# Ends of a kernel's four stages: without GpSimd's drain and without the second meeting of the engines, and one clear of semaphores moved into a stage

## The chip, the cores and the metric

The kernel runs on one core of a Trainium2 chip. Its five engines are TensorE (PE in the profile; PEld is its weight load), VectorE (DVE), ScalarE (ACT), GpSimd (POOL) and SyncE (SP, which here only issues transfers). A name with a q behind it (POOLq, PEldq) is that engine's sequencer: branches, waits, drains and semaphore operations, which are not counted as busy. The metric is device time in microseconds (us) of one execution. The span is the part of it from the first to the last instruction in the profile.

## What is computed

Two layers run over a stream `x` of 16 batches of 112 rows and 256 columns, with a context of 16 batches of 375 rows:

```python
x = x + L0_xattn(layernorm(x), ctx)          # 16 heads: attention over x itself and over the context, gated
x = x + L0_ffn(layernorm(x))                 # 8 experts (256 -> 512 -> 256), the best one for each row
x = x + L1_xattn(ctx, ctx, layernorm(x))     # one head of 256 over the context
x = x + L1_ffn(layernorm(x))                 # 16 experts (256 -> 1024 -> 256), 112 places each
```

A feed-forward layer sends each row to the expert with the largest router value. In the last layer an expert takes at most 112 rows.

## The kernel before, in words

`program` runs four functions, one after the other, as stages: `attention0`, `ffn0`, `attention1` and `ffn1`. Each allocates semaphores, opens a Block, and writes in it one list of instructions per engine. Inside a stage the engines meet only through semaphores: a producer adds to one, a consumer waits for a count. The stream `x` stays on chip (`xs`), so that what goes from stage to stage through memory is rows sorted by expert: `sorted0`, `made0` and `sorted1`.

- `attention0` (Block at L329) goes through the batches one by one, with five steps more than there are batches, since each engine works on another batch. GpSimd scatters the normed rows of each batch to `sorted0` with an indirect transfer (L1244), and waits for the last of them at L1250. At its end VectorE works out which expert owns each of 21 tiles (`owner_i`, `offset_i`, L739 to L748) and adds a row for the next attention (L752). SyncE loads weights for all that comes next. TensorE ends with dummy multiplications (`keep_busy`, L156).
- `ffn0` (Block at L1359) goes over 21 tiles of 128 rows. SyncE reads an offset (L1364) and loads the tile (L1370). TensorE turns it (L1478), multiplies it up (L1493) and down (L1506). GpSimd turns the row numbers into whole numbers (L1404) and scatters the result to `made0` (L1411). SyncE also loads eight blocks of weights for `ffn1`. At the end GpSimd and SyncE both wait for the last scatters, and SyncE then loads the first batch of `made0` for the stage behind (L1393). TensorE ends with 24 dummy multiplications.
- `attention1` (Block at L1549) goes over the batches again. VectorE adds `made0` to the stream (L1703) and norms it. GpSimd first makes constants (L1166 to L1175), later scatters rows to `sorted1` (L1244). At the end SyncE waits for the last scatter and then loads the rows of the first two experts (L1591), still inside the stage, since their buffers are outside it. TensorE ends with 22 dummy multiplications.
- `ffn1` (Block at L1872) goes over 16 experts. TensorE turns the rows (L1973), multiplies up (L1988) and down (L2002), VectorE forms the output rows (L1954), and GpSimd scatters them to the output (L1919) and at last waits for the last two of these transfers (L1924 and L1925).

```python
        def phase(run, *args):

            g.phase_sems = []
            run(*args)
            if g.used_sems:
                nc.clear_and_free_semaphores(g.used_sems)
            nc.all_engine_barrier()
            g.used_sems, g.phase_sems = g.phase_sems, None
```

Nothing plans the order of the work: it is the order of the lists. Each of SyncE's transfers is issued in its order behind the waits that stand ahead of it there, and GpSimd's indirect transfers have a queue of their own.

Of the kernel before, what the change touches and what calls it, by code (L numbers as in the profile page):

```python
# [124 lines left out]
def program(nc, a, out):  # L125
    with ExitStack() as ctx:
        g = Shared()
        g.nc = nc

        def sb(name, shape, dt=F32, where=ctx):  # L130
            return where.enter_context(nc.sbuf_tensor(name, shape, dt))
# [4 lines left out]
                g.phase_sems.append(handle)  # L136
            return handle

        g.phase_sems, g.used_sems = None, []

        def phase(run, *args):

            g.phase_sems = []
            run(*args)
            if g.used_sems:
                nc.clear_and_free_semaphores(g.used_sems)  # L146
            nc.all_engine_barrier()  # L147
            g.used_sems, g.phase_sems = g.phase_sems, None

        def dram(name, shape, dt=F32):  # L150
            return nc.dram_tensor(name, shape, dt, kind="Internal").ap()
# [42 lines left out]
        with ExitStack() as layer0:  # L194
            g.w1 = sb("w1", [P, E0, 2, F0], F32, layer0)
            g.stacks = sb("stacks", [P, 3, STACK], F32, layer0)
            g.b1 = sb("b1", [P, E0, F0 // P], F32, layer0)
            g.owner_i = sb("owner_i", [1, TILES], I32, layer0)
            g.offset_i = sb("offset_i", [1, TILES], I32, layer0)
            ffn0_views(g)  # L200
            phase(attention0, nc, a, g)
            phase(ffn0, nc, a, g)
        g.x_first = [sb(f"e1_x_in{k}", [C1, ROW1]) for k in range(2)]
        phase(attention1, nc, a, out, g)
        phase(ffn1, nc, a, out, g)

def ffn0_views(g):

    k2 = F0 // P  # L210
    late = g.stacks[:, 1:3, :].rearrange("p s n -> p (s n)")
    g.w2 = late[:, 0:E0 * k2 * D].rearrange("p (e k d) -> p e k d", e=E0, k=k2)
    last = g.stacks[:, 0, :]
    at = 0

    def part(words, pattern=None, **sizes):
        nonlocal at
        view = last[:, at:at + words]
        at += words
        assert at <= STACK  # L220
        return view.rearrange(pattern, **sizes) if pattern else view

    g.weights = {n: part(2 * D, "p (k d) -> p k d", k=2) for n in ("Wk", "Wv", "Wq", "Wo")}
    g.b2 = part(E0 * D, "p (e d) -> p e d", e=E0)
    g.b1_rows = part(P)[0:E0 * k2, :]
    g.bq, g.bv = part(2), part(2)

def attention0(nc, a, g_):
# [3 lines left out]
    with ExitStack() as phase:  # L233
# [92 lines left out]
        s_ctx = [sem(f"ctx_loaded{p}") for p in range(2)]  # L326
        s_stack = [sem(f"stack_ready{p}") for p in range(3)]
        s_mr = [sem(f"max_ready{p}") for p in range(2)]
        block = phase.enter_context(nc.Block())  # L329

        def copy_queries(engine, b, part):
            for t in range(NT):
# [998 lines left out]
def ffn0(nc, a, g):  # L1331
# [3 lines left out]
    with ExitStack() as phase:  # L1335
# [5 lines left out]
        with ExitStack() as tiles:  # L1341
# [14 lines left out]
            def tile_steps(engine, step):  # L1356
                steps(engine, step, TILES, 6, TILES - 3, end, 4)

            block = nc.Block()  # L1359
            with block:  # L1360
                @block.sync
                def _(sp):
# [33 lines left out]
                def _(pool):  # L1396
                    def step(j):
# [7 lines left out]
                        if (j - 1).real():  # L1405
# [6 lines left out]
                                                    in_=y[n.parity][:, :], in_offset=None, bounds_check=N - 1,  # L1412
                                                    oob_is_err=False).then_inc(s_out[n.parity], 16)

                    tile_steps(pool, step)
                    pool.wait_ge(s_out[0], 16 * ((TILES + 1) // 2))
                    pool.wait_ge(s_out[1], 16 * (TILES // 2))
# [95 lines left out]
def attention1(nc, a, out, g):  # L1513
# [3 lines left out]
    with ExitStack() as phase:  # L1517
# [28 lines left out]
        minus_wg = sb("minus_wg", [P, 2, E1])  # L1546
        expd, sums = sb("expd", [T, E1]), sb("sums", [T, 1])
        r = batch_routing(nc, g, phase, E1, C1, "r1", lambda n: bank[7][0:T, n.rows(E1)], s["logits_mm"], bank[6][0:T, 2 * T:2 * T + E1], acc, s["expd"], 4)
        block = nc.Block()  # L1549
        with block:  # L1550
            @block.sync
            def _(sp):
# [304 lines left out]
def ffn1(nc, a, out, g):  # L1857
# [7 lines left out]
    with ExitStack() as experts:  # L1865
        def tb(name, shape, dt=F32):
            return [g.sb(f"e1_{name}{p}", shape, dt, experts) for p in range(2)]
# [1 line left out]
        x_in = g.x_first + [g.sb(f"e1_x_in{k}", [C1, ROW1], F32, experts) for k in (2, 3)]  # L1869
        index = [g.sb(f"e1_index{k}", [C1, 1], I32, experts) for k in range(4)]  # L1870
        xt, hid, y = tb("xt", [P, 2, C1]), tb("hid", [P, KF, C1]), tb("y", [C1, D])
        block = nc.Block()  # L1872
        with block:  # L1873
            @block.sync
            def _(sp):
# [148 lines left out]
```

## Time and profile before

| what | value |
|---|---|
| time of the kernel, median of 3 runs | 772.79 us (769.84 to 773.85) |
| time of the profiled execution | 771.14 us |
| its span, from the first to the last instruction | 769.3 us |
| TensorE busy | 720.3 us, 94% of the span |
| VectorE, ScalarE, GpSimd busy | 419.7, 325.5 and 218.0 us |
| mean granted TensorE clock, as a share of full speed | 0.971 |

The profiled execution is one of its own. Busy time counts an engine's work, not its waits. A line of a group of instructions has the shortest, the median and the longest duration in nanoseconds, and the starts of the first and the last one in microseconds from the start of the span. A line of the timeline has the start and the duration in microseconds, and in brackets how long the engine had been idle and what released it.

### The profile page before, as it was taken

To read this page: it belongs to the slowest core of one execution; us is meant where nothing else is said; L and a number is where in the kernel's file an instruction comes from. 1 tells how busy PE (TensorE), PEld (TensorE's weight loads), DVE (VectorE), ACT (ScalarE), POOL (GpSimd) and SP (SyncE) were. 2 spreads that over 40 slices of the span, in tenths; PEclk is the share of its full clock that TensorE was granted. 3 is DMA by queue.
4 is the path that set the end of the run, shared out by engine and by line. 5 is a ranking of instruction groups with operands and counts; after the bars stand their busy time and mean duration, and the time that the engine had idled before them with its cause. 6 is when DMAs were issued, how large, how long until landed. Compare 5 with 4: busy or idle time off the path is not lost. (4 is left out here: it accounts for less than half of the span.)

```text
span 769.3 us, 19472 instructions
## 1 busy us (share of the span) xinstructions
PE 720.3 (94%) x6739; PEld 569.3 (74%) x6740; DVE 419.7 (55%) x1269; ACT 325.5 (42%) x884; POOL 218.0 (28%) x359
## 2 busy tenths in 40 slices
PE   5789999999999999999997898998999989999995
PEld 4457667777667776667665698997788878999994
DVE  4556877778877778776763322222588861111111
ACT  1335665555665556655553143331455540110110
POOL 3212333313333213243110023333356531111111
PEclk8979999999999999999999799999999998999998
DMA  6737554345653446642535459853566633999950
GB/s 173 197 98 195 139 144 107 91 126 166 173 150 103 126 139 174 170 124 74 177 117 156 123 184 259 212 171 104 168 202 217 198 105 111 309 327 342 332 160 17
DMA packets 99527, 128.12 MB, mean 167 GB/s; under 512 B 23394, under 2 KB 84683, under 8 KB 99312
## 3 DMA queue, kind: packets, MB, share of 16 engines
q1 hardware_dynamic: 90193, 115.07, 51.2%
q0 software_dynamic: 3824, 8.46, 3.6%
q10 hardware_dynamic: 5423, 3.48, 1.9%
q8 instruction: 50, 0.82, 0.5%
q14 instruction: 37, 0.30, 0.1%
HBM read 74.68 MB, written 23.88 MB: 128 GB/s over the span
## 5 line engine op out<-in xcount | busy, mean ns | idle before, releaser
L564 ACT ACTIVATE probs<-psum 128x448 f32<-128x448 f32 (+2 forms) x256 | 125.2, 541 | 57.9 <-PE psum L917 57.4
L776 DVE TENSOR_REDUCE neg_max<-psum 112x2 f32<-112x750 f32 x128 | 118.7, 928 | 6.5 <-PE psum L900 4.7
L900 PE MATMUL psum<-stacks 96*128 96x487 bf16 (+1 forms) x256 | 75.5, 377 | 4.6 <-DVE neg_max L777 2.6
L917 PE MATMUL psum<-stacks 102*128 102x112 bf16 (+1 forms) x1024 | 76.9, 214 | 1.6 <-ACT probs L564 0.4
L932 PEld LDWEIGHTS psum<-probs,rings 128*32 128x32 f32 (+2 forms) x2048 | 44.9, 109 | 45.2 <-issue 36.8
L917 PEld LDWEIGHTS psum<-stacks 102*128 102x128 bf16 (+1 forms) x1024 | 54.4, 98 | 30.4 <-ACT probs L564 23.8
L932 PE MATMUL psum<-probs,rings 128*32 128x112 f32 (+2 forms) x2048 | 75.8, 265 | 0.0
L1954 DVE SCALAR_TENSOR_TENSOR e_y<-psum,e_x_in 112x256 f32<-112x256 f32 x16 | 7.7, 484 | 98.0 <-PE psum L2002 98.0
L1988 PEld LDWEIGHTS psum<-e_xt,rings 128*128 128x128 f32 x512 | 59.5, 192 | 2.2 <-ACT e_xt L1934 1.3
L1988 PE MATMUL psum<-e_xt,rings 128*128 128x112 f32 x512 | 59.7, 275 | 0.9 <-ACT e_xt L1934 0.9
L2002 PE MATMUL psum<-rings,e_hid 128*112 128x256 f32 x256 | 57.9, 379 | 1.3 <-DVE e_hid L1961 1.3
L987 PE MATMUL psum<-rings 128*128 128x375 f32 x128 | 48.3, 500 | 5.6 <-ACT xt L575 5.6
L2002 PEld LDWEIGHTS psum<-rings,e_hid 128*112 128x112 f32 x256 | 44.0, 177 | 10.4 <-issue 1.7
L777 DVE TENSOR_REDUCE neg_max<-psum 112x2 f32<-112x224 f32 x128 | 48.4, 378 | 0.0
L1934 ACT COPY e_xt<-psum 128x224 f32<-128x224 f32 x16 | 5.5, 345 | 99.9 <-PE psum L1973 99.9
L1438 ACT ACTIVATE t_hid<-psum,b 128x128 f32<-128x128 f32 x84 | 26.2, 363 | 50.9 <-PE psum L1493 50.9
L1493 PEld LDWEIGHTS psum<-t_xt,t_w 128*128 128x128 f32 x336 | 41.9, 197 | 5.7 <-issue 3.7
L1493 PE MATMUL psum<-t_xt,t_w 128*128 128x128 f32 x336 | 42.8, 283 | 3.4 <-issue 2.7
L1919 POOL DMA_INDIRECT out<-e_y,e_index x16 | 15.2, 951 | 98.7 <-issue 52.8
L444 POOL TENSOR_TENSOR ln_rstd<-ln_mv,eps 112x1 f32<-112x1 f32 x16 | 3.0, 190 | 138.4 <-DVE ln_mv L647 138.4
L1411 POOL DMA_INDIRECT made<-t_y,t_index x21 | 24.2, 1151 | 59.0 <-issue 45.0
L1506 PE MATMUL psum<-stacks,t_hid 128*128 x168 | 40.5, 386 | 0.0
(228 smaller groups left out, 1392.3 us busy)
## 6 DMA issues: line engine op xcount, KB each, us to landing
rings<-in_L_ffn_w SPq DMA_DIRECT2D x32, 1024.0 KB, 7.7
stacks<-rings SPq DMA_DIRECT2D x96, 243.5 KB
ct_dram<-rings SPq DMA_DIRECT2D x16, 375.0 KB, 4.9
a_ct<-ct_dram SPq DMA_DIRECT2D x16, 375.0 KB, 4.4
a_ctx<-in_ctx SPq DMA_DIRECT2D x16, 375.0 KB
stacks<-q_parts SPq DMA_DIRECT2D x93, 56.0 KB
rings<-in_ctx SPq DMA_DIRECT2D x16, 256.0 KB
w<-in_L_ffn_W SPq DMA_DIRECT2D x8, 512.0 KB, 6.2
```

The source lines that it names most:

```text
L564: nc.scalar.activation(probs[k % 4][0:keys, :, :], src, ACT.Exp, scale=DH ** -0.5).then_inc(s["exp_done"], 1)
L776: nc.vector.tensor_reduce(neg_max[:, 0, h:h + 2], psum[0:T, pair:pair + 2, 0:S], AX, ALU.max, negate=True)
L777: nc.vector.tensor_reduce(neg_max[:, 1, h:h + 2], psum[0:T, pair:pair + 2, S:KV], AX, ALU.max, negate=True).then_inc(s["max_done"], 1)
L900: last = nc.tensor.matmul(bank[2 - 2 * (k % 2) + j][0:rows, 0:KV], q_flat[n.third][0:QK, h * T:h * T + rows], k_stack[n.third][0:QK, h, :] ...
L917: last = nc.tensor.matmul(bank[4 + k % 2][0:wide, j * T:(j + 1) * T], k_flat[n.third][:, first:first + wide], q_stack[n.third][:, h, :], s ...
L932: last = nc.tensor.matmul(bank[6 + g // 2][32 * j:32 * j + 32, col:col + T], v[n.parity][0:keys, chunk, h, :], probs[k % 4][0:keys, j, :], ...
L987: last = nc.tensor.matmul(bank[(0, 3)[h]][:, 0:S], w_p[:, a_, 2, h, :], ct[b.parity][:, a_, :], start=(a_ == 0), stop=(a_ == 1))
L1438: nc.scalar.activation(hid[j.parity][:, f, :], up_bank(j, f)[:, f % 2 * P:(f % 2 + 1) * P], ACT.Relu, bias=bias).then_inc(s["hid"], 1)
L1493: last = nc.tensor.matmul(up_bank(j, f)[:, f % 2 * P:(f % 2 + 1) * P], w1_now[j.parity][:, k, f * P:(f + 1) * P], xt2[j.parity][:, k, :], ...
L1506: last = nc.tensor.matmul(bank[6 + n.parity][:, 0:D], hid[n.parity][:, f, :], w2[:, bass.ds(e, 1), f, :].rearrange("p o d -> p (o d)"), st ...
L1988: last = nc.tensor.matmul(bank[2 * e.parity + f // 4][:, f % 4 * C1:(f % 4 + 1) * C1], g.ring1[e.quarter][:, k, f * P:(f + 1) * P], xt[e.p ...
L2002: last = nc.tensor.matmul(bank[6 + n.parity][0:C1, 0:D], hid[n.parity][:, f, :], g.ring2[n.quarter][:, f, :], start=(f == 0), stop=(f == K ...
```

## The change

```diff
@@ program
-        g.phase_sems, g.used_sems = None, []
-
-        def phase(run, *args):
-
-            g.phase_sems = []
-            run(*args)
-            if g.used_sems:
-                nc.clear_and_free_semaphores(g.used_sems)
-            nc.all_engine_barrier()
-            g.used_sems, g.phase_sems = g.phase_sems, None
+        g.phase_sems = None
...
-            phase(attention0, nc, a, g)
-            phase(ffn0, nc, a, g)
+            g.phase_sems = g.first_sems = []
+            attention0(nc, a, g)
+            g.phase_sems = None
+            ffn0(nc, a, g)
         g.x_first = [sb(f"e1_x_in{k}", [C1, ROW1]) for k in range(2)]
-        phase(attention1, nc, a, out, g)
-        phase(ffn1, nc, a, out, g)
+        attention1(nc, a, out, g)
+        ffn1(nc, a, out, g)
@@ attention0
-        block = phase.enter_context(nc.Block())
+        block = phase.enter_context(nc.Block(no_gpsimd_drain=True))
@@ ffn0
-            block = nc.Block()
+            block = nc.Block(no_gpsimd_drain=True)
...
+                    nc.clear_and_free_semaphores(g.first_sems)
                     tile_steps(pool, step)
@@ attention1
-        block = nc.Block()
+        block = nc.Block(no_gpsimd_drain=True)
@@ ffn1
-        block = nc.Block()
+        block = nc.Block(no_gpsimd_drain=True)
```

## Rows read from the trace of the kernel before

**Rows 1.** The page's first part: busy time, share and instructions of each engine.

```profile
PE 720.3 (94%) x6739; PEld 569.3 (74%) x6740; DVE 419.7 (55%) x1269; ACT 325.5 (42%) x884; POOL 218.0 (28%) x359
```

**Rows 2.** Windows, last three stages: from:to, length, each engine's busy time, clock, DMA.

```profile
432.30:527.40 95.10, 89.42 (x606) 83.22 (x606) 23.54 (x42) 31.84 (x105) 28.28 (x42) 0.96 0.62 178
527.40:643.40 116.00, 107.61 (x748) 92.14 (x748) 78.52 (x352) 53.12 (x193) 54.22 (x102) 0.97 0.55 167
643.40:769.35 125.95, 116.76 (x804) 105.91 (x804) 16.32 (x32) 12.76 (x32) 18.30 (x32) 0.98 0.74 241
```

**Rows 3.** Line L233, window 429 to 434: end of `attention0`, its first meeting.

```profile
L233 PEldq DRAIN  x1: 5042/5042/5042, 427.1 to 427.1; - x1
...
L233 POOLq DRAIN  x1: 1380/1380/1380, 430.4 to 430.4; - x1
...
L233 SPq EVENT_SEMAPHORE  x1: 17/17/17, 432.3 to 432.3; - x1
```

**Rows 4.** Line L147, window 429 to 434: the second meeting behind `attention0`.

```profile
L147 SPq EVENT_SEMAPHORE  x1: 17/17/17, 432.6 to 432.6; - x1
```

**Rows 5.** Timeline, start of `ffn0`.

```profile
433.62 7.19 SPq L1370 DMA_DIRECT2D t_in<-sorted  x6
...
435.91 0.18 POOL L1404 CAST t_index<-t_in 128x1 int32<-128x1 f32 x1 [7.37 <-DMA t_in<-sorted]
```

**Rows 6.** Line L1360, window 524 to 529: end of `ffn0`, its first meeting.

```profile
L1360 PEldq DRAIN  x1: 2175/2175/2175, 524.9 to 524.9; - x1
...
L1360 POOLq DRAIN  x1: 1774/1774/1774, 525.4 to 525.4; - x1
...
L1360 SPq EVENT_SEMAPHORE  x1: 17/17/17, 527.4 to 527.4; - x1
```

**Rows 7.** Line L146, window 526 to 529: GpSimd clears `attention0`'s semaphores.

```profile
L146 POOLq DRAIN  x1: 223/223/223, 527.4 to 527.4; - x1
L146 POOLq EVENT_SEMAPHORE_RANGE_CLEAR  x1: 614/614/614, 527.7 to 527.7; - x1
```

**Rows 8.** Line L147, window 524 to 529: the second meeting behind `ffn0`.

```profile
L147 SPq EVENT_SEMAPHORE  x1: 17/17/17, 528.5 to 528.5; - x1
```

**Rows 9.** Timeline, end of `ffn0` and start of `attention1`.

```profile
525.31 0.36 SPq L1393 DMA_DIRECT2D empty<-made  x1
...
528.63 0.42 DVE L1703 TENSOR_TENSOR xs<-xs,empty 112x256 f32<-112x256 f32 x1 [6.34 <-PEq L147]
```

**Rows 10.** Tile `empty`, window 520 to 535: its two loads' time to landing.

```profile
DMA to landing us min/median/max: 2.0/2.8/3.6
```

**Rows 11.** Line L1550, window 640 to 645: end of `attention1`, its first meeting.

```profile
L1550 PEldq DRAIN  x1: 2173/2173/2173, 641.0 to 641.0; - x1
...
L1550 POOLq DRAIN  x1: 1374/1374/1374, 641.9 to 641.9; - x1
```

**Rows 12.** Timeline, end of `attention1` and start of `ffn1`.

```profile
641.68 0.79 SPq L1591 DMA_DIRECT2D e_x_in<-sorted  x2
...
644.02 0.68 PE L156 MATMUL psum<-ident 128*128 128x128 f32 x4 [0.90 <-PEq L147]
...
644.55 0.18 POOL L1912 CAST e_index<-e_x_in 112x1 int32<-112x1 f32 x1 [4.50 <-DMA e_x_in<-sorted]
```

**Rows 13.** Line L1873, window 765 to 770: end of `ffn1`, its first meeting.

```profile
L1873 POOLq EVENT_SEMAPHORE  x2: 17/17/17, 768.4 to 768.5; - x2
...
L1873 POOLq DRAIN  x1: 1372/1372/1372, 767.0 to 767.0; - x1
L1873 SPq EVENT_SEMAPHORE  x1: 17/17/17, 768.6 to 768.6; - x1
```

**Rows 14.** Line L147, window 765 to 770: the second meeting behind `ffn1`.

```profile
L147 PEldq EVENT_SEMAPHORE  x1: 51/51/51, 769.3 to 769.3; - x1
```

**Rows 15.** Windows as in rows 2: two stretches at the lower granted clock.

```profile
437.50:440.90 3.40, 2.75 (x15) 2.35 (x13) 0.69 (x1) 1.51 (x5) 0.00 (x0) 0.50 0.30 83
...
632.10:638.90 6.80, 6.80 (x34) 6.80 (x35) 3.15 (x23) 1.57 (x7) 1.92 (x2) 0.50 0.12 35
```

## The prediction

> **What bounds the kernel now.** I read the page's first part first. TensorE is busy for 94% of the span [rows 1], so that only an idle stretch of it, or the time behind its last work, can be won without making its work shorter. The windows by stage say the same of the last three stages: it is busy for 89.4 of 95.1, 107.6 of 116.0 and 116.8 of 126.0 us [rows 2]. Nothing inside a stage is edited but one clear of semaphores, so each stage's length stays if its start moves as a whole. What I must read, then, is each of the four ends: when the last engine arrives at the meeting, when it is released, and what the next stage's first work waits for besides that release.
>
> The first end is late because of TensorE, not GpSimd. GpSimd's drain begins at 430.4 and takes 1.38 us, to 431.8, while TensorE's ends at 427.1 + 5.04 = 432.1. The release is at 432.3 [rows 3], the second one at 432.6 [rows 4]. SyncE's first load of `ffn0` goes out at 433.6, and GpSimd, idle for 7.37 us, gets that tile at 435.9 [rows 5]. The second end has both drains level: GpSimd 525.4 + 1.77 = 527.2, TensorE 524.9 + 2.18 = 527.1, release 527.4 [rows 6]. Then the sequencer of GpSimd drains for 0.22 us and clears for 0.61 us [rows 7], and the second release comes at 528.5 [rows 8]. VectorE starts `attention1` 0.1 us behind it, at 528.63, and the trace names the meeting as what it waited for [rows 9]. The third end has the drains level again: 641.0 + 2.17 = 643.2 and 641.9 + 1.37 = 643.3 [rows 11]. Here the loads for `ffn1` were issued at 641.68, ahead of both meetings, and GpSimd's first work there waits for that load, not for a meeting, until 644.55 [rows 12]. At the last end nothing follows: GpSimd's drain begins at 767.0 and takes 1.37 us, release 768.6 [rows 13], and the last instruction of the kernel is the second meeting's, from 769.3 to 769.35 [rows 14].
>
> **The change part by part.** *First end.* The drain of 1.38 us goes, but TensorE's still ends at 432.1, so it is worth nothing. The second meeting goes: 432.6 - 432.3 = 0.3 us [rows 3, 4]. The new kind of meeting is not in the trace. Its nearest row is the exchange of the old one: GpSimd's two semaphore operations begin 0.1 us apart, and SyncE is released 0.1 us behind [rows 13]. If a plain drain can't itself add to the semaphore and a separate operation must, that is one such step more, 0.1 us; if it is leaner, up to 0.1 us less. I take half a step more, since drain and count were one instruction before: gain 0.25 us, between 0.2 and 0.4. The load of the first tile waits for nothing but the release, so the gain moves all of `ffn0`.
>
> *The moved clear.* It now stands in GpSimd's list ahead of the first tile. Its price is that of the rows behind `ffn0`, 0.22 + 0.61 = 0.84 us [rows 7], or less by the drain. Behind it on GpSimd is queued the wait for the first tile, and for that tile the engine idles 7.37 us [rows 5], of which 435.9 - 432.6 = 3.3 us lie behind the release. So 0.84 us is hidden at least three times over, and I cost it at nothing. Without that cover it would delay only GpSimd's row numbers, which are needed for its own scatters. It issues no transfer and passes no queue of SyncE's.
>
> *Second end.* The drain: 0.1 us between the two engines, about what a further step costs, so nothing. The clear and the second meeting: 528.5 - 527.4 = 1.1 us [rows 6, 8]. What is late next? The first batch of `made0` is loaded from 525.31 [rows 9], and loads into that buffer take 2.0 us at the least [rows 10]. It has thus landed at 527.3 if it is that one, just ahead of the release at 527.4. I take the whole 1.1 us; if it took the median's 2.8 us it would land at 528.1 and only 0.4 us would be won, but VectorE's wait was put down to the meeting and not to the load. Bounds 0.4 and 1.25 us. All loads of `attention1` are issued behind the release and move with it.
>
> *Third end.* Clear and second meeting are worth some 0.5 us on paper, since TensorE's dummy multiplications start at 644.02, 0.8 us behind the end of the drains [rows 11, 12]. But the rows land when they land: their load is issued inside the stage, and GpSimd gets them only at 644.55. Cover: the load's flight, 641.68 to about 644.5. I cost it at a gain of nothing, upper bound 0.2 us, because the dummies would be out of the way when the rows land.
>
> *Last end.* From the start of GpSimd's drain at 767.0 to the last instruction's end at 769.35 are 2.35 us. Of this the exchange of one meeting stays, 768.6 - 768.4 = 0.2 us [rows 13, 14]. Gain 2.15 us, with half a step more for the new meeting 2.1. No work and no transfer is in its way: the last output has landed before the drain begins. Bounds 2.0 and 2.2 us.
>
> **Sum.** 0.25 + 0 + 1.1 + 0 + 2.1 = 3.45, say 3.5 us. Against the profiled execution's own 771.14 us, of which 1.8 us lie outside its span of 769.3, that gives 767.6 us. The median of the runs shown lies 1.65 us above that execution, so on the scale of the medians I forecast 772.79 - 3.5 = 769.3 us. The unknown costs put the gain between 0.2 + 0.4 + 0 + 2.0 = 2.6 and 0.4 + 1.25 + 0.2 + 2.2 = 4.05 us. By about 0.5%, 3.9 us, a measurement of this kernel can tell a change from none, so the forecast sits just inside that, and most of what is uncertain is on which side it falls. The three runs shown are themselves 4 us apart.
>
> **A drain that is only put off.** No row shows what follows the span; 1.8 us of the profiled time lie around it. If GpSimd's engine has to finish what its drain did before the execution counts as over, 1.37 us [rows 13] comes back outside the span: gain 3.5 - 1.4 = 2.1 us, time 770.7. For it: the drain took 1.37 to 1.77 us at each of the four ends [rows 3, 6, 11, 13], even where the last transfer had landed, so it is work of its own and not a wait for data. Against it: the meeting's own releases need no such drain, and the only drain of GpSimd shown right behind a long one took 0.22 us [rows 7], so that most of the cost may go with the kind of drain and not with the engine's state. Chance 0.15. The Trainium skill, Runtime: NRT & Kernel Launch, section The ~15µs preamble/postamble breakdown, puts a meeting of all engines and a reset of the DMA rings behind every kernel. By that rule a drain left out could be paid there; no row here shows it.
>
> **The release is not what the next stage waits for.** If at the first two ends a transfer sets the start, as it does at the third, the 1.35 us of these two vanish and only the last end's 2.1 us are won: 770.7. The third end speaks for it [rows 12]; that VectorE starts 0.1 us behind the release [rows 8, 9] and that `ffn0`'s load is issued behind it speak against it. Chance 0.1.
>
> **TensorE's clock.** The granted clock was 0.50 of full, the 1.2 GHz level, in two stretches among others: 3.4 us, a few microseconds into `ffn0`, and 6.8 us at the end of `attention1`, where TensorE had short idle gaps between small products [rows 15]. In the second one 34 products kept it busy for 6.8 us, 0.20 us each, against 0.144 over the stage [rows 2, 15]. By the level itself such a stretch costs at most half its length, and that only where TensorE sets the pace. Moved starts can move these stretches. If the one in `ffn0` no longer falls on products, up to 1.7 us more is won: gain 5.2, time 767.6; chance 0.1. The other way is the case on the slow side. Place: the start of `ffn1`, where the dummies now end earlier, while the rows land when they did, so that TensorE idles some 0.5 us more in one piece just ahead of its longest run of products. Price: a stretch as long as the two of [rows 15] together, 10.2 us, at half clock, 5.1 us lost, less the 3.5 won: 1.6 us slower, 774.4. It decides from 7 us of low clock on, at which 3.5 us are lost. Against it: total idle there doesn't grow, it only moves, and the clock was full in that place before. Chance 0.05. The Trainium skill, TensorE: Matmul & The Clock Gate, Part 1, says that recent activity decides the clock, and by that rule alone the shorter gaps at the first two ends could only help.
>
> **The change doesn't do what it says.** The option could leave a drain of GpSimd in place, or the meeting through semaphores could cost as much as the old two. Then only the clears go: about 0.8 us at the second end and 0.4 at the last, time 771.6. Chance 0.05.
>
> **How the numbers follow.** Forecast 0.55, put-off drain 0.15, transfers set the start 0.1, clock for it 0.1, clock against it 0.05, no effect 0.05. The range holds forecast and both cases at 770.7, the bounds of the sum (768.7 to 770.2), the favourable clock at 767.6, and some 1 us of scatter of a median on both sides; it leaves out the slow side and part of the favourable clock: 766.8 to 771.9. Faster by over 0.5% is below 768.9: two fifths of the forecast's 0.55, nearly all of the 0.1 of the favourable clock, and 0.05 of the rest through scatter, 0.37. Slower by over 0.5%: half of the unfavourable clock and scatter, 0.04. The rest, 0.59, is within.
>
> **What would show it right or wrong.** Right: GpSimd's sequencer has no drain of over 1 us at any of the four ends; TensorE's drains of 5.0, 2.2 and 2.2 us are still there; one meeting per end; `ffn0` starts its first load 0.25 us earlier against TensorE's drain; VectorE's first addition of `attention1` follows that drain by 0.4 to 0.5 us in place of 1.5; `ffn1`'s first product does not follow its load's issue sooner; from GpSimd's wait for the last output to the last instruction 0.4 us in place of 2.5. The span shrinks by 3.5 us and the time outside it stays at 1.8. Wrong: the time outside the span grows by over 1 us (the put-off drain), VectorE's first addition waits for its load, GpSimd's first row numbers of `ffn0` come later than its tile, or the granted clock at the start of `ffn1` is 0.5.

## The result, and the profile after

The changed kernel takes 768.35 us, the median of 12 runs (766.89 to 770.67), against 772.0 us for 12 runs of the kernel before (768.65 to 777.28). The ratio is 0.9956, 95% interval 0.9934 to 0.9977: 3.4 us less, between 1.8 and 5.1. A second set of 12 runs, further down, gave 0.9968 (0.9949 to 0.9988). The profiled execution took 767.21 us, with a span of 765.4 (765.36): 1.8 us outside it, as in the profiled execution before.

Line numbers in the kernel after differ: the first stage's end is L226 (L233 before), the moved clear L1408, the ends of `ffn0`, `attention1` and `ffn1` are L1353, L1544 and L1867, the dummy products L147, the last wait for an output L1919.

The first end, for [rows 3, 4, 5]: the instructions of L226, of the moved clear L1408, and the timeline of the start of `ffn0`.

```profile
L226 PEldq EVENT_SEMAPHORE  x2: 51/51/51, 431.7 to 431.9; - x2
L226 POOLq EVENT_SEMAPHORE  x2: 17/17/17, 431.8 to 431.9; - x2
L226 PEldq DRAIN  x1: 5162/5162/5162, 426.4 to 426.4; - x1
...
L226 POOLq COMPARE_BRANCH  x1: 38/38/38, 429.6 to 429.6; - x1
...
L226 SPq EVENT_SEMAPHORE  x1: 17/17/17, 431.9 to 431.9; - x1
...
L1408 POOLq DRAIN  x1: 217/217/217, 431.9 to 431.9; - x1
L1408 POOLq EVENT_SEMAPHORE_RANGE_CLEAR  x1: 614/614/614, 432.2 to 432.2; - x1
...
432.91 2.58 SPq L1363 DMA_DIRECT2D t_in<-sorted  x3
...
434.97 0.44 PE L1472 MATMUL psum<-ident,t_in 128*128 128x128 f32 x2 [1.37 <-DMA t_in<-sorted]
435.09 0.18 POOL L1397 CAST t_index<-t_in 128x1 int32<-128x1 f32 x1 [7.21 <-DMA t_in<-sorted]
```

GpSimd has no drain at L226. TensorE's drain still ends the wait, at 426.4 + 5.16 = 431.6. A second thing is new in the rows: TensorE now has two semaphore operations there. Its drain no longer adds to the semaphore itself; an operation of its own does so at 431.7, and the release follows at 431.9. So SyncE's release has ended 0.32 us behind TensorE's drain, where it was 0.17 before. GpSimd's clear is over at 432.8, 2.3 us ahead of its first row numbers.

The second end, for [rows 6, 8, 9].

```profile
L1353 PEldq DRAIN  x1: 2173/2173/2173, 524.7 to 524.7; - x1
...
525.11 0.36 SPq L1386 DMA_DIRECT2D empty<-made  x1
...
527.26 0.42 DVE L1697 TENSOR_TENSOR xs<-xs,empty 112x256 f32<-112x256 f32 x1 [5.19 <-PEq L1353]
```

VectorE begins 0.40 us behind the end of TensorE's drain (526.87), where it was 1.54 before. It still waits for the meeting and not for its rows, which were asked for 2.15 us earlier.

The third end, for [rows 11, 12]: the timeline of the end of `attention1` and the start of `ffn1`, first two rows of before that [rows 12] leaves out, then the kernel after.

```profile
644.54 0.36 PE L1973 MATMUL psum<-ident,e_x_in 112*128 112x112 f32 x2
...
645.34 0.92 PE L1988 MATMUL psum<-e_xt,rings 128*128 128x112 f32 x6 [0.43 <-ACT e_xt L1934]
```

```profile
639.46 0.79 SPq L1585 DMA_DIRECT2D e_x_in<-sorted  x2
...
642.17 0.68 PE L147 MATMUL psum<-ident 128*128 128x128 f32 x4 [0.42 <-PEq L1544]
642.54 0.18 POOL L1906 CAST e_index<-e_x_in 112x1 int32<-112x1 f32 x1 [4.71 <-DMA e_x_in<-sorted]
...
642.69 0.36 PE L1967 MATMUL psum<-ident,e_x_in 112*128 112x112 f32 x2
...
643.49 0.92 PE L1982 MATMUL psum<-e_xt,rings 128*128 128x112 f32 x6 [0.43 <-ACT e_xt L1928]
```

Here something moved that I had held fixed. TensorE's last dummies end at 641.76, 2.3 us behind the issue of the row load; before it was 1.45 us (643.13 against 641.68). So the meeting came later as seen from the load, and the first expert product (L1982, at 643.49) follows the load's issue by 4.02 us, against 3.66 before. In both kernels TensorE goes from its four dummies to the rows (L1973, L1967) without an idle gap, 0.52 us behind the dummies' start, and the first expert product stands 1.3 us behind that start. So what TensorE waits for here is the meeting that releases the dummies, before the change too; the wait for the load in [rows 12] is GpSimd's.

The last end, for [rows 13, 14]: first GpSimd's last wait for an output before, then the rows after.

```profile
L1925 POOLq EVENT_SEMAPHORE  x1: 17/17/17, 766.8 to 766.8; - x1
```

```profile
L1919 POOLq EVENT_SEMAPHORE  x1: 17/17/17, 764.9 to 764.9; - x1
...
L1867 POOLq EVENT_SEMAPHORE  x2: 17/17/17, 765.2 to 765.3; - x2
...
L1867 PEldq EVENT_SEMAPHORE  x1: 51/51/51, 765.3 to 765.3; - x1
```

From GpSimd's last wait to the last instruction it is 0.42 us, against 2.55 before.

The windows of the last three stages, for [rows 2], and of the low clock, for [rows 15]; columns as there.

```profile
431.90:527.10 95.20, 89.62 (x606) 83.37 (x606) 23.57 (x42) 31.85 (x105) 27.92 (x42) 0.96 0.64 177
527.10:642.10 115.00, 107.44 (x748) 92.16 (x748) 78.62 (x352) 53.13 (x193) 54.25 (x102) 0.97 0.56 171
642.10:765.36 123.26, 116.75 (x804) 105.91 (x804) 16.34 (x32) 12.76 (x32) 18.27 (x32) 1.00 0.76 244
437.10:443.90 6.80, 6.15 (x29) 5.75 (x28) 0.69 (x1) 2.43 (x9) 0.00 (x0) 0.50 0.68 203
```

TensorE's busy times in the stages are those of before to 0.2 us. The low clock of `ffn0`'s start is there again, at 1.2 GHz for 6.8 us in place of 3.4.

The whole span, taken apart at events that both traces have:

| stretch | before | after | difference |
|---|---|---|---|
| to the end of TensorE's drain behind `attention0` | 432.15 | 431.60 | -0.55 |
| first end: to the issue of `ffn0`'s load | 1.47 | 1.31 | -0.17 |
| `ffn0`, to the end of TensorE's drain | 93.47 | 93.96 | +0.49 |
| second end: to VectorE's first addition | 1.54 | 0.40 | -1.15 |
| `attention1`, to the load of `ffn1`'s rows | 113.05 | 112.20 | -0.85 |
| third end: from that load to the first product | 3.66 | 4.02 | +0.37 |
| `ffn1`, to the last wait | 121.46 | 121.46 | 0 |
| last end | 2.55 | 0.42 | -2.14 |
| sum | 769.35 | 765.36 | -3.99 |

The four ends give -3.1 us. The other -0.9 lies outside them. `ffn0`'s stretch alone lay anywhere from 88.9 to 94.0 us in the 12 profiles in which it starts with this load (x7 and x8 load that tile earlier), so no single pair of spans can size this change. Much of that is TensorE's clock. The five profiles with 6.8 us at 1.2 GHz inside `ffn0` have 93.2 to 94.0 us (before, after, x6, x9, x10), x3 with 3.4 us has 90.7, and the six without any have 88.9 to 92.2. The change itself, profiled a second time (x12), had none:

```profile
431.00:522.40 91.40, 86.71 (x606) 80.27 (x605) 23.56 (x42) 31.85 (x105) 27.98 (x42) 1.00 0.65 185
```

TensorE was busy there for 2.9 us less with the same 606 products, and the execution took 764.34 us.

### The profile page after: what moved, and what is told of

Read it like the earlier page. It is cut to its first block and busy times, and to the rows that moved or that the text cites. A ratio compares the mean times of both kernels' runs of the same rounds, so it can differ in the third digit from the quotient of the medians.

```text
span 765.4 us, 19436 instructions
## 1 busy us (share of the span) xinstructions
PE 722.6 (94%) x6739; PEld 570.5 (75%) x6740; DVE 420.1 (55%) x1269; ACT 325.7 (43%) x884; POOL 217.6 (28%) x359
## 5 line engine op out<-in xcount | busy, mean ns | idle before, releaser
L1982 PEld LDWEIGHTS psum<-e_xt,rings 128*128 128x128 f32 x512 | 59.5, 192 | 2.2 <-ACT e_xt L1928 1.3
L1982 PE MATMUL psum<-e_xt,rings 128*128 128x112 f32 x512 | 59.7, 275 | 0.9 <-ACT e_xt L1928 0.9
```

What stands on the lines that cost most here:

```text
L1982: last = nc.tensor.matmul(bank[2 * e.parity + f // 4][:, f % 4 * C1:(f % 4 + 1) * C1], g.ring1[e.quarter][:, k, f * P:(f + 1) * P], xt[e.p ...
```

## The experiments

My theory: the gain is the sum of what the ends show, and a drain left out is gone. The rivals: the drain is paid elsewhere, or the start of the next stage hangs on a transfer. Each ratio is against the kernel before on the same chip: 770.63 us (34 runs) beside x1 to x4, 770.0 (17 runs) beside x5, x6, x8 and x9, and 770.69 (17 runs) beside x7, x10, x11 and x12.

### Only the drain, only the meetings, only the last end

```diff
# x1: the kernel before, at its four Blocks
-with nc.Block() as block:
+with nc.Block(no_gpsimd_drain=True) as block:
# x2: the kernel after, at its four Blocks
-with nc.Block(no_gpsimd_drain=True) as block:
+with nc.Block() as block:
# x3: the kernel before, at the last stage only
-phase(ffn1, nc, a, out, g)
+g.phase_sems = []
+ffn1(nc, a, out, g)      # its Block with no_gpsimd_drain=True
```

> Before, with GpSimd's drain left out at all four ends and the second meetings and clears kept. Theory (only what lies behind the last arrival counts): the first three ends gain nothing, since TensorE's drain ends level with GpSimd's, and the new meeting costs 0.15 us more from TensorE's drain to the release (0.32 against 0.17 at the first end). The last end gains 1.4 us less 0.1. Total 1.0 to 1.3 us less than before, and each release 0.3 us behind TensorE's drain. Rival (the drain is only put off): the long drain of 1.4 us turns up in the short one at L147 or L146, and the time does not move by more than 0.3 us; or the time outside the span grows from 1.8 to over 3 us.

> After, with GpSimd's drain back in all four Blocks; no second meeting, clears as in after. Theory: from the end of TensorE's drain to the start of the next stage 0.2 us at the first and the second end in place of 0.5 and 1.4, and at the last end 1.4 us of drain stay: from GpSimd's last wait to the end 1.8 us in place of 2.55. Total 0.3 + 1.1 + 0.75 = 2.2 us less than before. Rival (what sets the next stage's start is a load): the second end gains 0.5 us or less, total 1.5. Together with the kernel without drains alone the gains should add up to after's 3.1 to 3.6 us; if GpSimd's drain were hidden or put off everywhere, this one would have all of after's gain.

> Before, with the last stage alone changed: its Block without GpSimd's drain, and neither clear nor second meeting behind it. Theory: the first three ends read as before, the last is 2.1 us shorter (0.4 us from GpSimd's last wait to the end of the span), total 2.1 us less. Rival (the work is paid outside the span): the span shrinks by 2.1 us but the time outside it grows by over 1 us, so the total is 1 us less or not at all.

x1 measured 770.61 us, ratio 0.9996 (0.9973 to 1.0018). x2 measured 768.52, 0.9958 (0.994 to 0.9977). x3 measured 767.93, 0.9963 (0.9942 to 0.9983). The ratios are those of the measurement side by side; the quotient of two medians differs from them by up to 0.0015.

x1 was the surprise. The drains of GpSimd in its trace are, first, at the second meeting of the first end, and then in the clear of the last end:

```profile
L147 POOLq DRAIN  x1: 1371/1371/1371, 431.5 to 431.5; - x1
...
L147 SPq EVENT_SEMAPHORE  x1: 17/17/17, 433.0 to 433.0; - x1
```

```profile
L146 POOLq DRAIN  x1: 115/115/115, 762.7 to 762.7; - x1
```

The 1.37 us have not gone. They stand in the next drain that GpSimd makes, the plain one of the second meeting, which took 34 ns there before. So it is not the kind of drain that costs: a plain one takes as long when it is the first behind the transfers. In the profile before they lay under TensorE's long drain; now all engines wait for them: from TensorE's drain to `ffn0`'s load it is 2.83 us in place of 1.47. The last end wins 1.40 us (1.15 in place of 2.55), since the drain that comes with its clear takes 0.12. Together +1.36 - 1.40 = 0, as timed. At the two ends between them the clear's drain comes first and is as short as ever.

x2 keeps the four drains and still wins what x1 does not. At the third end the drain lies under TensorE's, at the first two it ends 0.12 and 0.14 us behind it. At the last end nothing covers it, and there x2 wins 0.44 of the 2.14 us, where 0.75 were expected: GpSimd's two semaphore operations lie 0.41 us apart in that meeting, in place of 0.08.

```profile
L1353 PEldq DRAIN  x1: 2173/2173/2173, 523.6 to 523.6; - x1
...
L1353 POOLq DRAIN  x1: 1781/1781/1781, 524.2 to 524.2; - x1
...
L1867 POOLq DRAIN  x1: 1356/1356/1356, 765.7 to 765.7; - x1
```

By its rows x2's ends win 0.2, 1.1 and 0.44 us, 1.7 together, and its third end gave back 0.55 in that one profile. The ratio says 3.2 us (1.8 to 4.6), so that the timing found rather more than the rows show, and does not tell x2 from the full change; what the rest is stays open. x3 wins the last end's 2.13 us, all of it inside the span, with 1.7 us outside it. That speaks against a payment after the span. Its interval holds 2.1 us. By time alone x2 and x3 can't be told from the full change, whose intervals theirs overlap; what tells them apart is the rows.

x3 shows one thing more. It keeps the drain at the first end, and there GpSimd's drain, not TensorE's, ended last, by 0.42 us (433.29 against 432.87):

```profile
L234 PEldq DRAIN  x1: 4423/4423/4423, 428.4 to 428.4; - x1
...
L234 POOLq DRAIN  x1: 1376/1376/1376, 431.9 to 431.9; - x1
```

GpSimd comes to the first meeting once its last scatter has landed. In the 14 profiles that was from 1.8 us before to 0.6 us behind the end of TensorE's drain. My estimate from these arrivals and the drain's 1.38 us: with the drain GpSimd would have ended last in nine of the 14, and the drain would have cost 0 to 1.38 us there, some 0.5 us on average. In x1's own profile GpSimd arrived 0.1 us before the end of TensorE's drain, so that the +1.36 us above compares it with a profile in which GpSimd came early.

### Where the drain's time comes from

If a plain drain of GpSimd costs something for each indirect transfer since the last drain, then it can be made short by a drain that comes with a clear, and long by letting transfers add up. Four kernels, one execution each:

```diff
# x9: x1, with a clear of one spare semaphore ahead of the first end's second meeting
+            else:
+                nc.clear_and_free_semaphores([nc.alloc_semaphore(name="spare")])
             nc.all_engine_barrier()
# x6: the kernel after, a meeting with plain drains added behind attention1
         attention1(nc, a, out, g)
+        nc.all_engine_barrier()
# x11: x6, with a clear of one spare semaphore ahead of that meeting
+        nc.clear_and_free_semaphores([nc.alloc_semaphore(name="spare")])
+        nc.all_engine_barrier()
# x10: the kernel after, the last Block with its drain
-with nc.Block(no_gpsimd_drain=True) as block:
+with nc.Block() as block:
```

> The kernel without GpSimd's drains alone, with a clear of one unused semaphore ahead of the second meeting of the first end, where there was none. In that kernel the long drain came back there, 1.37 us at the second meeting, but not at the three ends that have a clear. Theory (GpSimd's first plain drain behind a scatter costs 1.4 us, and the short drain that belongs to a clear takes that cost away for 0.1 to 0.2): the drain ahead of the clear takes 0.2 us, the plain one of the meeting 0.05, and TensorE's drain to the first load of ffn0 is 1.7 to 1.9 us in place of 2.8. Rival (the first end is long for another reason: it is the first drain of all, or its place in time): the plain drain still takes 1.37 us, the stretch is 2.8 to 3.1 us.

> After, with a second meeting back at the third end alone, without a clear. Theory (a plain drain costs 1.4 us wherever the last scatter has not been followed by a drain): GpSimd drains for 1.4 us in that meeting, from TensorE's drain to the first product of ffn1 it is 3.3 to 3.5 us in place of 1.7. Rival (a meeting costs 0.33 us, as those of before did): 2.0 us. Third reading (the rows' load covers everything there): 1.7 us or less and 3.6 us from the load's issue, whatever the meeting takes.

> After with a clear of one unused semaphore and a second meeting at the third end, where the second meeting alone had GpSimd drain for 3.09 us. Theory (the drain that belongs to a clear ends the count and costs only by its own size): 0.07 us for it and 0.04 us for the plain drain behind it, 37 scatters or not; from TensorE's drain to the first product of ffn1 2.2 to 2.5 us in place of 5.7. Rival (the drain of the clear pays what is owed when that is more than one stage's): 3 us in the first of the two drains.

> After with GpSimd's drain back at the last end alone. The plain drains so far: 1.37 to 1.38 us behind 16 scatters, 1.77 behind 21, 3.09 behind 37 (a plain drain at the third end with none at the second). Theory (a plain drain costs about 84 ns for each indirect transfer since GpSimd's last drain of any kind, wherever these lie): 21 + 16 + 16 = 53 transfers, 4.4 to 4.5 us, and from the last wait to the end of the span 5.1 us. Rival (each stage's own scatters count, or the third end's 3.09 us were a chance): 1.37 us, and 2.1 us to the end.

x6 came out by neither its theory nor its rivals: its drain took 3.09 us and not 1.4, and from TensorE's drain to the first product of `ffn1` it was 5.69 us, not 3.3 to 3.5. The count of transfers was read from it, and x11 and x10 then tested it. The drains of the four, in the order x9, x6, x11, x10; each kernel's instructions of the line:

```profile
L148 POOLq DRAIN  x1: 74/74/74, 431.7 to 431.7; - x1
L148 POOLq EVENT_SEMAPHORE_RANGE_CLEAR  x1: 47/47/47, 431.8 to 431.8; - x1
...
L149 POOLq DRAIN  x1: 39/39/39, 431.8 to 431.8; - x1
```

```profile
L198 POOLq DRAIN  x1: 3092/3092/3092, 641.9 to 641.9; - x1
```

```profile
L198 POOLq DRAIN  x1: 53/53/53, 640.8 to 640.8; - x1
...
L199 POOLq DRAIN  x1: 52/52/52, 641.0 to 641.0; - x1
```

```profile
L1867 POOLq DRAIN  x1: 4398/4398/4398, 765.4 to 765.4; - x1
```

Since the last drain of any kind GpSimd had issued 16 indirect transfers at a drain of 1.37 us, 21 at one of 1.77 [rows 6], 21 + 16 = 37 at one of 3.09 (x6) and 21 + 16 + 16 = 53 at one of 4.40 (x10). That is 86, 84, 84 and 83 ns for each. A drain that comes with a clear does not pay it (74 ns behind 16 transfers in x9, 53 ns behind 37 in x11), and the plain drain behind it has nothing left to pay (39 and 52 ns). Counted in rows (112 each, 128 in `ffn0`) the first two would be 0.77 and 0.66 ns, so that the transfers fit better. The number of GpSimd's engine instructions does not fit at all: `attention1` has 102 and `ffn1` 32 [rows 2], and both left 1.37 us [rows 11, 13].

By their rows x9 has 1.68 us from TensorE's drain to `ffn0`'s load, in place of x1's 2.83 (1.7 to 1.9 expected), x11 has 2.13 us from TensorE's drain to `ffn1`'s first product, in place of x6's 5.69 (2.2 to 2.5 expected), and x10 has 4.85 us from the last wait to the end (5.1 expected), in place of 0.42. That is 4.4 us given back, more than the four ends had won. The single times are 771.16 (x9), 773.59 (x6), 766.52 (x11) and 771.95 us (x10); one execution says little where those of one kernel spread by 7 us. x9 and x6 both had a stretch at 1.2 GHz at the start of `ffn1`, which then took 123.1 and 123.7 us in place of 121.46. In x6 TensorE was idle for 3.7 us ahead of it; columns of the second fence as in [rows 15]:

```profile
645.30 1.20 PE L147 MATMUL psum<-ident 128*128 128x128 f32 x4 [3.71 <-PEq L198]
```

```profile
645.20:652.00 6.80, 6.27 (x28) 5.95 (x29) 0.00 (x0) 0.34 (x1) 0.50 (x3) 0.50 0.12 37
```

This is my rival on the clock, in its place; the 6.8 us cost 2.2. x9 and x1 had the same idle stretch there, 1.18 us, and x1 kept the full clock. In the change itself, where TensorE is idle for 0.42 us at that meeting, it did not come in either profile.

### What covers the moved clear

```diff
# x5: the kernel after, behind the moved clear, four fills of 128x256
+                    for k in range(4):
+                        pool.memset(late[:, k, :], 0.0)
```

> After, with four fills of 128x256 on GpSimd (about 1.7 us each, of memory that nobody reads) behind the moved clear in ffn0: the clear's place made eight times as costly, 0.8 to some 7.5 us. Theory (the clear is covered): GpSimd's first row numbers come at 439 in place of 435, its first scatter waits for VectorE as before, and the stretch from the first tile's load to TensorE's drain at the end of ffn0 stays within what it varies by anyway (88.9 to 94.0 us in six profiles), with the first steps of ffn0 3.1 to 4.8 us each. Rival (GpSimd is on the way there): the second or third step is 3 us longer, because SyncE's loads wait for the row numbers.

The test was weaker than planned: the four fills took 2.16 us together, not 7. I had priced one by the only fill of that size in the kernel before, which took 1.70 us (L1279).

```profile
432.15 2.16 POOL L1411 MEMSET t_late<- 128x256 f32 x4 [3.96 <-DMA sorted<-r_rows,r_place_i]
...
434.28 0.44 PE L1475 MATMUL psum<-ident,t_in 128*128 128x128 f32 x2 [1.41 <-DMA t_in<-sorted]
434.39 0.19 POOL L1398 CAST t_index<-t_in 128x1 int32<-128x1 f32 x1
...
443.81 1.02 POOL L1405 DMA_INDIRECT made<-t_y,t_index  x1 [8.09 <-DVE t_y L1463]
```

With 2.2 us more behind the clear GpSimd arrives together with the tile, and the first scatter still waits 8.1 us for VectorE's rows. The time was 763.84 us and the span 762.1 us (one execution), and `ffn0`'s stretch 91.0 us. The cover of the 0.84 us is real in this profile: clear and fills, 3.0 us together, just fit under the tile's arrival. How much more it holds was not tried.

### What the next stage waits for

```diff
# x4: the kernel after, fewer dummy products at the end of ffn0 and of attention1
-24 and 22
+18 and 16
# x7: the kernel after, ffn0's first tile loaded by SyncE inside attention0, into a free part of the weight ring
+            sp.wait_ge(s["table_step"], 14)
+            sp.wait_ge(s["pv_done"], 16 * B)
+            for p in range(2):
+                sp.wait_ge(r.scattered[p], 16 * B // 2)
+            at = sp.value_load(g_.offset_i[0:1, 0:1], min_val=0, max_val=E0 * REGION)
+            sp.dma_start(g_.tile0, g_.sorted0[bass.ds(at, P), :]).then_inc(g_.s_tile0, 16)
...
-                    for c in range(4):
+                    for c in range(1, 4):
# x8: x7 and x4 together
# x12: the kernel after, unchanged, for comparison beside x7
```

> After, with 18 in place of 24 dummy multiplications at the end of ffn0 and 16 in place of 22 at the end of attention1. In after TensorE's drain ends last at both ends, and at the third one the dummies now run 0.15 us past the landing of the rows. Theory: TensorE's drain ends 1.3 us earlier at both. The second end then waits for the first load of made0, which lands at about the release: gain 0 to 0.2 us. The third end waits for its load: first product 3.6 us behind the load's issue in place of 4.0: gain 0.2 to 0.4. Total 0.3 to 0.5 us less than after. Rival (the clock): TensorE's longer idle piece brings the 1.2 GHz level into the start of attention1 or ffn1, and the time rises by 1.5 to 3.5 us.

> After, with the fewer dummies (18 and 16) and with the first tile of ffn0 loaded inside attention0 into a part of the weight ring that is free by then, once the last scatter has landed and VectorE has worked out the offset; the other tiles as before. Theory (what is left of the first end is the tile's flight and its offset read behind the release): from TensorE's drain at the first end to the first product of ffn0, 4.3 us in after, it becomes 2.2 to 2.6 us, set by VectorE's copy of the weights, and the total is 1.7 to 2.5 us less than after, about 764.5 to 766.5 where before is 771. Rival (the gain is hidden elsewhere: the second tile's load or the weights are late next, or SyncE arrives last at the meeting): the second step is longer by what the first one won, total as after or 0.5 us less.

> After with the first tile of ffn0 loaded inside attention0, and all dummies as in after. Theory: from TensorE's drain at the first end to the first product of ffn0 2.7 us, as with fewer dummies, in place of 4.3; the rest as after, ffn1's stretch from its first product to the last wait 121.5 us. Total 1.6 us less than after in the same comparison. Rival (fewer dummies were the better half): total as after.

> After once more, beside the kernel with the early tile on the same chip: ratio to before 0.995 to 0.997, 3.1 us of it from the ends, and the readings of the four ends as in the first profile: 1.3, 0.4 and 1.7 us from TensorE's drain to the next stage's first work, 0.4 us from the last wait to the end.

x4: 766.92 us, 0.9946 (0.9924 to 0.9968), not to be told from the kernel after, so the 0.3 to 0.5 us expected can't be tested by the time. With the dummies out of the way the second end moves to the load, as the waits in its timeline say:

```profile
524.02 0.36 SPq L1386 DMA_DIRECT2D empty<-made  x1
...
526.05 0.42 DVE L1697 TENSOR_TENSOR xs<-xs,empty 112x256 f32<-112x256 f32 x1 [5.07 <-DMA empty<-made]
```

VectorE begins 2.03 us behind the load's issue, against 2.16 in the kernel after: only 0.13 us is left before the transfer is the bound. With 18 dummies SyncE, which issues that load late, is the last to arrive at the meeting. At the third end TensorE now waits for the rows themselves:

```profile
641.34 0.41 PE L1967 MATMUL psum<-ident,e_x_in 112*128 112x112 f32 x2 [0.71 <-DMA e_x_in<-sorted]
```

The first product came 3.61 us behind the load. In the four profiles in which TensorE waits for the rows (x4, x7, x8, x10) it was 3.5 to 3.8 us; that is the floor that the landing sets. Before (3.66) and x1 (3.59) lie at the same value, but there the meeting set it and the rows were just in time. Where TensorE's dummies end later against the load it is more: x2 had 4.21 us, x12 4.15, and x3, with both meetings kept there, 4.77.

x7: 764.06 us (6 runs), 0.9921 (0.9894 to 0.9948), beside x12's 768.33, 0.9968 (0.9949 to 0.9988), on the same chip. Its first end:

```profile
429.99 0.37 SPq L439 DMA_DIRECT2D rings<-sorted  x1
...
430.92 1.58 PE L147 MATMUL psum<-ident 128*128 128x128 f32 x12 [0.42 <-PEq L228]
...
432.33 0.38 PE L1486 MATMUL psum<-ident,rings 128*128 128x128 f32 x2
...
433.22 0.35 PE L1501 MATMUL psum<-t_xt,t_w 128*128 128x128 f32 x1 [0.51 <-ACT t_xt L1433]
```

The load is issued ahead of the meeting, and from TensorE's drain to `ffn0`'s first product it is 2.7 us, against 4.3 in the kernel after and 4.5 in x12. These 1.6 to 1.8 us are what the trace shows; the rest of the 4.3 us between the medians is not traced to an edit, and with six runs it may be scatter. 1.6 us had been expected. By its median it is the fastest version here.

x12 is the change once more: from TensorE's drain to the next stage's first work 1.44, 0.40 and 1.70 us, and 0.42 at the last end, as expected but for the first. There GpSimd's last scatter landed late, and GpSimd came to the meeting behind TensorE (branch at 430.3, TensorE's drain over at 430.17).

x8: 766.54 us, 0.995 (0.9922 to 0.9978), 3.5 us below its kernel before, where some 4.5 to 6.5 were expected. It has x7's first end (2.69 us), but its profile shows two stretches at 1.2 GHz that the kernel after's does not, 3.4 us each, at 527.5 early in `attention1` and at the start of `ffn1`, both behind ends with fewer dummies. `ffn1` took 1.5 us longer:

```profile
640.10:643.50 3.40, 3.22 (x15) 3.22 (x16) 0.00 (x0) 0.13 (x1) 0.37 (x2) 0.50 0.25 73
```

## Why the prediction was right

The forecast was 769.3 us against 772.79, a ratio of 0.9955; measured were 0.9956 and 0.9968. That the gain came out at 3.4 us for 3.5 is partly luck: the intervals are 1.8 to 5.1 and 0.9 to 3.9 us, wider than the errors of the steps. What tests the steps is the rows:

- **First end**, 0.25 us: the load follows TensorE's drain by 0.17 us less. In x12 it was 0.03 us less, since GpSimd arrived last. TensorE's drain ended last in the profile that I read, so there the drain was worth nothing, but that was luck of that execution: x2 and x3 show GpSimd's drain ending last by 0.1 and 0.4 us, and by my estimate above it was worth some 0.5 us on average. VectorE too arrives only 0.1 us ahead of TensorE at this end. The second meeting's 0.3 us went, and the new meeting takes 0.15 us more than the old exchange (0.32 behind the drain in place of 0.17), more than the half step that I took, for the reason that I had named: a separate operation adds to the semaphore.
- **Moved clear**, nothing: GpSimd was done with it 2.3 us ahead of its tile, and x5 shows 3.0 us covered in its one profile.
- **Second end**, 1.1 us: 1.15 in the profiles (1.54 in place of 0.40), and the doubt about the load was fair, since it is 0.13 us from being the bound.
- **Third end**, nothing: the term that failed, if by little. I read the end from GpSimd's wait for the load [rows 12], but TensorE, which sets the pace of `ffn1`, did not wait for the rows there; it waited for the meeting. My cover, "the load's flight, 641.68 to about 644.5", took the dummies' end as fixed against the load. It is not: their end came 1.1 to 2.7 us behind the load's issue in the profiles with 22 dummies. With one meeting the first product follows TensorE's drain by 1.6 to 1.7 us when the dummies are late (after 1.71, x2 1.59, x12 1.70), with two by 2.1 to 2.2 (x3 2.09, before 2.19). So the second meeting's 0.4 to 0.5 us is won there when the dummies come last, and nothing when the rows do; before, the rows were ready just as TensorE came to them. Set against the kernel before this is chance: +0.37 us in this pair.
- **Last end**, 2.1 us: 2.14, and alone worth 2.13 (x3).
- **Sum**: 3.1 us by the ends, 3.5 predicted, 3.4 and 2.5 timed.

**The put-off drain.** For the change as made the forecast held: the time outside the span was 1.8 us in the profile after (1.7 to 2.2 in all profiles), not the 3 us of the rival. Over all executions it was 1.9 us on average in the change's 24 and 1.7 in the 68 of before. These 0.2 us don't go with the missing drain: x3, without it, had 1.7, and x10, with it, 1.9. What they are stays open. The Trainium skill, Runtime: NRT & Kernel Launch, section The ~15µs preamble/postamble breakdown, puts work of its own behind every kernel; no run showed a GpSimd drain move into it. But inside the span the rival was right: x1 shows a drain that is put off and paid in full, and x6 and x10 show it growing. The change escapes it for a reason that I did not see: the moved clear at the head of `ffn0` has a short drain that ends the first stage's 16 transfers, and no plain drain comes after the later ones. My argument against the rival, the 0.22 us drain [rows 7], was no argument: it stood behind a drain that had already paid, and x1 shows that the cost goes with what GpSimd has issued, not with the kind of drain.

**Transfers set the start**: false at the first two ends, near at the second. **The clock**: the favourable case came in one of the change's two profiles, x12, where `ffn0` had no stretch at 1.2 GHz; but seven kernels besides had none either, x1 with all its meetings among them, and the mean granted clock was 0.971 and 0.973 over the change's two sets of runs and 0.972 to 0.973 over those of before. So it is no gain of the change. The unfavourable case exists (x6, x8, x9) and cost 1.5 to 2.2 us, but came only in other kernels, not in the profiles of the change. **No effect**: false.

Unedited stages differ by microseconds from run to run, and part of it goes with the clock: of the 34 executions of the kernel before beside x1, the seven with a mean granted clock of 0.975 or more have a median of 769.6 us, the ten with 0.969 or less one of 772.3. Why the clock differs from run to run, and what the rest is, stays open.

## What to carry to other kernels

At the end of a stage ask which engine's drain ends last: only there does a shorter drain win time. Ask it in more than one profile, since an engine that waits for a transfer arrives early in one execution and late in the next. Asking for the next stage's first tile ahead of the meeting won 1.6 us here, the leaner meeting 0.2 at the same end. An option that leaves a drain out must be read together with the next drain on that engine, for the work may be waiting there; a clear of semaphores placed where the engine idles ended it here. Where executions scatter by several microseconds, size an edit of one by the distance between two events in the trace, and use the timed ratio for the sign.

## What the runs showed of the hardware

- GpSimd's plain drain took 1.37, 1.77, 3.09 and 4.40 us behind 16, 21, 37 and 53 indirect transfers, though GpSimd had waited for the last of them before (x10): some 84 ns for each since the last drain.
- The drain that comes with a clear took 0.05 to 0.22 us whatever had been issued (53 ns with one semaphore behind 37 transfers, 217 ns with the first stage's semaphores behind 16), and left nothing for the next plain drain. The clear itself took 47 ns for one semaphore and 614 for the first stage's.
- One meeting without such a drain took 0.29 to 0.32 us from the end of the last engine's drain to the end of the release, at the first three ends of the kernel after. The old one, whose drains add to the semaphore themselves, took 0.17 us at the first end.
- GpSimd's arrival at the first meeting, which hangs on its last scatter's landing, lay from 1.8 us before to 0.6 us behind the end of TensorE's drain in 14 profiles.
- Without any stretch at 1.2 GHz in `ffn0` its 606 products kept TensorE busy for 86.7 us (x12), with 6.8 us of it for 89.6 (after).
- At the start of `ffn1` the granted clock fell to 1.2 GHz behind an idle stretch of TensorE of 3.7 us (x6), behind two of 1.6 and 0.6 us with fewer dummies (x8), and once with all dummies and both meetings (x9, idle for 1.2 us). x1 with the same 1.2 us, and x4, with as few dummies as x8, kept the full clock there. What decides it stays open.
